# A graph-attention and mixture-of-experts layer: GpSimd normalises the rows of the first four routed blocks, and x is loaded in three pieces

## What is computed

```
sim  = tanh(adj * adj) where adj > 0            # adj is 4096 x 4096, float32
keep the 350 largest of each row of sim         # only rows with more than 350 positives change
h2   = tanh(layernorm(x) @ W_proj + b_proj)
x    = x + relu(new_adj @ (h2 @ W_gcn) + b_gcn)

n      = layernorm(x)
scores = n @ Wg.T + bg ; the two best experts ; softmax over their two scores
x      = x + sum over the two of  p_e * (relu(n @ W1[e].T + b1[e]) @ W2[e].T + b2[e])
```

## Time and profile before

| | us |
|---|---|
| runs | 513.41, 513.22, 513.01; median 513.22 |
| the profiled execution, its own time | 511.21 |
| its span | 509.4 |
| PE busy | 410.6 (81%) |
| DVE busy | 370.3 (73%) |
| ACT busy | 338.9 (67%) |
| POOL busy | 247.0 (48%) |

### The profile page before, as it was taken

The page is one execution under the profiler, slowest core; times in us unless marked ns, Lnnn a source line. Parts: engine busy times, 40 slices in busy tenths (PEclk is TensorE's granted clock), DMA queues, the critical chain, the costliest instruction groups (busy, mean ns, idle before and its releaser), DMA issues.

```text
span 509.4 us, 8989 instructions
## 1 busy us (share of the span) xinstructions
PE 410.6 (81%) x2671; PEld 256.7 (50%) x2672; DVE 370.3 (73%) x889; ACT 338.9 (67%) x345; POOL 247.0 (48%) x355
## 2 busy tenths in 40 slices
PE   0799999999898899999749999410999898989900
PEld 0455444444443445544334444210899898988900
DVE  4978899989999996696769999751555555554526
ACT  1789999799979876999757798100466555554500
POOL 2059941005206738718615875551266656564620
PEclk9999999999999999999978999855899999998975
DMA  8649589786666677586544781013233223232149
GB/s 242 266 146 378 219 286 374 251 283 245 222 243 213 227 264 284 188 292 272 196 181 129 278 314 69 31 43 121 77 88 96 82 62 92 64 86 65 40 155 339
DMA packets 31128, 95.56 MB, mean 188 GB/s; under 512 B 5532, under 2 KB 18132, under 8 KB 22896
## 3 DMA queue, kind: packets, MB, share of 16 engines
q1 hardware_dynamic: 19904, 80.06, 45.3%
q0 software_dynamic: 6048, 12.72, 7.5%
q10 hardware_dynamic: 5136, 2.30, 1.6%
HBM read 83.28 MB, written 12.67 MB: 188 GB/s over the span
## 4 chain that ended last, share of the span: by engine, by line
PE 21%; DVE 13%; issue 7%; DMA 4%; POOL 3%; SPq 2%; ACT 0%; POOLq 0%; DVEq 0%
DVE marks L820 5%; PE bank L1379 3%; PE bank L1380 3%; PE bank L1381 3%; PE bank L1400 3%; PE bank L1402 3%; PE bank L1401 3%; DMA tbuf<-expert_rows 2%; POOL expert_rows L602 2%; PE bank L1367 2%; POOL routed_rows L572 1%; DMA routed_rows<-aug,slots 1%; PE bank L1243 1%; SPq L422 1%; PE bank L1389 1%
## 5 line engine op out<-in xcount | busy, mean ns | idle before, releaser
L1269 PE MATMUL bank<-tbuf,g_sb 128*128 128x512 f32 x512 | 232.6, 602 | 1.7 <-ACT g_sb L1036 1.4
L1269 PEld LDWEIGHTS bank<-tbuf,g_sb 128*128 128x128 f32 x512 | 94.8, 192 | 108.9 <-issue 101.1
L820 DVE SCALAR_TENSOR_TENSOR marks<-abuf,marks 128x2048 bf16<-128x2048 int32 x56 | 128.3, 2291 | 1.2
L1016 ACT ACTIVATE tbuf<-abuf 128x2048 f32<-128x2048 f32 x64 | 121.4, 1897 | 3.5 <-PE bank L1269 2.7
L1020 ACT ACTIVATE tbuf<-tbuf 128x2048 f32<-128x2048 f32 x64 | 122.3, 1910 | 2.0
L602 POOL DMA_INDIRECT expert_rows<-abuf x78 | 76.7, 983 | 65.2 <-ACT abuf L1136 37.8
L572 POOL DMA_INDIRECT routed_rows<-aug,slots x64 | 83.7, 1308 | 50.4 <-DVE base L798 31.6
L982 DVE SCALAR_TENSOR_TENSOR tbuf<-bank,tbuf 128x512 f16<-128x512 f32 x78 | 51.8, 690 | 34.4 <-ACT tbuf L1130 34.4
L1130 ACT ACTIVATE tbuf<-bank 128x512 f16<-128x512 f32 x78 | 46.5, 597 | 44.5 <-PE bank L1381 43.1
L1400 PE MATMUL bank<-w2h,tbuf 128*128 x312 | 54.5, 220 | 0.0
L1401 PE MATMUL bank<-w2l,tbuf 128*128 x312 | 54.5, 220 | 0.0
(11 more groups left out here) (222 smaller groups left out, 510.8 us busy)
## 6 DMA issues: line engine op xcount, KB each, us to landing
abuf<-in_adj_tiles SPq DMA_DIRECT2D x64, 1024.0 KB, 5.2
abuf<-routed_rows SPq DMA_DIRECT2D x41, 130.0 KB, 2.1
wstage<-in_w POOLq DMA_DIRECT2D x16, 256.0 KB, 7.0
tbuf<-expert_rows SPq DMA_DIRECT2D x8, 512.0 KB, 6.9
out<-xres ACTq DMA_DIRECT2D x8, 256.0 KB, 6.2
expert_rows<-abuf POOLq DMA_INDIRECT x78
routed_rows<-pad SPq DMA_DIRECT2D x9, 130.0 KB, 2.5
routed_rows<-aug,slots POOLq DMA_INDIRECT x64
```

Of the source, the lines that this page charges most:

```text
L820: dve.scalar_tensor_tensor(mark, bits_in, 1.0, mark, ALU.min, ALU.add).then_inc(s_raw, 1)
L1016: act.activation(tbuf[:, n % NBUF, :, :], abuf[:, n % NBUF, :, :], ACT.Square).then_inc(s_sq, 1)
L1269: last = pe.matmul(ps_feat[ib % 2][:, :], g_sb[:, c, :], tbuf[:, buf, cc, :], start=(c == 0), stop=(c == C - 1))
```

## The change

Four edits are made.

- `normalise` and `cut_rows` take the engine as an argument. For the first four routed blocks GpSimd runs them, right behind `scale` of the same block and so ahead of `scatter` of the block before; for the last four blocks DVE runs them as before. Where DVE makes the scale itself (from the fifth block on) it first waits until the block before has been normalised.
- x is loaded in three pieces: 4, 8 and 20 column groups. The first two are issued ahead of adjacency chunk 0, the third behind it.
- At the start ACT and PE begin only group 0 ahead of chunk 0: ACT copies the turned group 0 ahead of the square of chunk 0 and its projection between square and tanh; PE turns only group 1 behind `gcn(0)`; `project(1)` and `turn_group(2)` stand behind chunk 0.
- The order of ACT's four small loads is changed (b_proj first), its table-loading activation reads `ident` and no longer waits for these loads, and PE waits for them only ahead of `project(0)`. A memset that only signals writes `need` in place of `tmp`, and `probabilities` gets the wait on the scatter of its `aug` buffer that `cut_rows` had on DVE.

```
-    PIECES = [(0, 3 * CK), (3 * CK, C)]
+    PIECES = [(0, CK), (CK, 3 * CK), (3 * CK, C)]
...
             load_x(0)
+            load_x(1)
             for n in range(NCH):
...
                 if n == 0:
-                    load_x(1)
+                    load_x(2)
...
             for i, b in enumerate(ORDER):
                 if i < POOLED:
                     scale(i, b, routed)
+                    normalise(pool, i, b, routed)
+                    cut_rows(pool, i, routed)
                 if i:
                     scatter(i - 1, routed)
...
                 if scale:
                     link(last)
+                    if i:
+                        dve.wait_ge(rs.xn, i)
                     last = norm_scale(dve, link, b * SUB, SUB)
...
             def probabilities(i, b, rs):
 
                 q = i % 2
+                if i >= 2:
+                    dve.wait_ge(rs.scat[q], i // 2 * Q * 16)
...
                     if n == START[i] + LATER[i] + AT_NORM:
-                        normalise(i, b, routed)
-                        cut_rows(i, routed)
+                        if i >= POOLED:
+                            normalise(dve, i, b, routed)
+                            cut_rows(dve, i, routed)
...
+            turned_out(0)
             square_chunk(0)
+            act.wait_ge(s_w, 64)
+            projected_out(0)
             tanh_chunk(0)
-            turned_out(0)
+            gcn_out(0)
             turned_out(1)
-            projected_out(0)
-            turned_out(2)
-            projected_out(1)
-            gcn_out(0)
...
+                if n == 0:
+                    projected_out(1)
+                    turned_out(2)
...
             turn_group(0)
+            pe.wait_ge(s_w, 64)
+            project(0)
+            gcn(0)
             turn_group(1)
-            project(0)
-            turn_group(2)
-            project(1)
-            gcn(0)
...
+                if n == 0:
+                    project(1)
+                    turn_group(2)
```

More of the change, by code:

```diff
@@ L382, in norm_scale, with normalise, cut_rows @@
             return last
+        def normalise(eng, i, b, rs):
+            eng.wait_ge(rs.ns, i + 1)
+            if i:
+                eng.wait_ge(rs.r2, i)
+                eng.wait_ge(rs.cut, 2 * i)
+            for cc in range(SUB):
+                c = b * SUB + cc
+                last = eng.tensor_scalar(nrm[:, cc, :], xres[:, c, :], mean[:, c:c + 1],
+                                         rstd[:, c:c + 1], ALU.subtract, ALU.mult)
+            last.then_inc(rs.xn, 1)
+        def cut_rows(eng, i, rs):
+            q = i % 2
+            if i >= 2:
+                eng.wait_ge(rs.scat[q], i // 2 * Q * 16)
+            if i == 0:
+                eng.wait_ge(s_one, 2)
+            eng.wait_ge(rs.xn, i + 1)
+            row = aug[:, q, 0, :, 0:D].bitcast(fp16)
+            eng.tensor_copy(row[:, :, 0:D - 1], nrm[:, :, 0:D - 1]).then_inc(rs.cut, 1)
+            eng.wait_ge(rs.cut, 2 * i + 1)
+            eng.tensor_tensor(row[:, :, D:2 * D - 1], nrm[:, :, 0:D - 1], row[:, :, 0:D - 1], ALU.subtract
+                              ).then_inc(rs.cut, 1)
         block = ctx.enter_context(nc.Block())
@@ L733, in add_features @@
                     link(last)
+                    if i:
+                        dve.wait_ge(rs.xn, i)
                     last = norm_scale(dve, link, b * SUB, SUB)
                 last.then_inc(rs.ns if scale else rs.st, 1)
-            def normalise(i, b, rs):
-                dve.wait_ge(rs.ns, i + 1)
-                if i:
-                    dve.wait_ge(rs.r2, i)
-                    dve.wait_ge(rs.cut, 2 * i)
-                for cc in range(SUB):
-                    c = b * SUB + cc
-                    last = dve.tensor_scalar(nrm[:, cc, :], xres[:, c, :], mean[:, c:c + 1],
-                                             rstd[:, c:c + 1], ALU.subtract, ALU.mult)
-                last.then_inc(rs.xn, 1)
-            def cut_rows(i, rs):
-                q = i % 2
-                if i >= 2:
-                    dve.wait_ge(rs.scat[q], i // 2 * Q * 16)
-                if i == 0:
-                    dve.wait_ge(s_one, 2)
-                dve.wait_ge(rs.xn, i + 1)
-                row = aug[:, q, 0, :, 0:D].bitcast(fp16)
-                dve.tensor_copy(row[:, :, 0:D - 1], nrm[:, :, 0:D - 1]).then_inc(rs.cut, 1)
-                dve.wait_ge(rs.cut, 2 * i + 1)
-                dve.tensor_tensor(row[:, :, D:2 * D - 1], nrm[:, :, 0:D - 1], row[:, :, 0:D - 1], ALU.subtract
-                                  ).then_inc(rs.cut, 1)
             def choose(i, b, rs):
@@ L883, in _ @@
                     write_features(early, 0)
-                    dve.memset(tmp[:, :], 0.0).then_inc(fixed_early, 1)
+                    dve.memset(need[:, :], 0.0).then_inc(fixed_early, 1)
                 for i, b in enumerate(ORDER):
@@ L941, in _ @@
                     add_features(b, b, rerouted, scale=True)
-                    normalise(b, b, rerouted)
-                    cut_rows(b, rerouted)
+                    normalise(dve, b, b, rerouted)
+                    cut_rows(dve, b, rerouted)
                     choose(b, b, rerouted)
@@ L1004, in _ @@
         def _(act):
+            act.dma_start(bp_sb[:, :], b_proj.rearrange("(p o) -> p o", o=1)).then_inc(s_w, 16)
             act.dma_start(wp_sb[:, :], w_proj).then_inc(s_w, 16)
             act.dma_start(wg_sb[:, :], w_gcn).then_inc(s_w, 16)
-            act.dma_start(bp_sb[:, :], b_proj.rearrange("(p o) -> p o", o=1)).then_inc(s_w, 16)
             act.dma_start(bg_sb[:, :], b_gcn.rearrange("(p o) -> p o", o=1)).then_inc(s_w, 16)
-            act.wait_ge(s_w, 64)
-            act.activation(ex[:, 0:1], bp_sb[:, 0:1], ACT.Tanh)
+            act.wait_ge(s_ident, 1)
+            act.activation(ex[:, 0:1], ident[:, 0:1], ACT.Tanh)
             def square_chunk(n):
@@ L1165, in _ @@
             pe.wait_ge(s_ident, 1)
-            pe.wait_ge(s_w, 64)
             def turn_group(g):
```

## The result

The changed kernel took 526.22 us (median of four, 523.79 to 529.38) where the kernel before took 513.12 beside it: a ratio of 1.026 (1.022 to 1.030), 13 us slower. I had said 513.6 and a range up to 517.0. The profiled execution took 525.71 with a span of 523.9, 14.5 more than before.

The account below looks back on a forecast made before the run. The stage was taken as often bound by DVE up to 320 us, with start, first two blocks and scatter deciding: -1.2 - 1.8 + 3.4 = +0.4, so 513.6 us as median; range 511.2 to 517.0.

Parts of the forecast that it names:

- the third block: Third routed block: forecast to change nothing, DVE spending its gained 4.43 wait on the next wait, for ACT's corrected rows.
- The start: Loading x in three pieces: -1.2 us at DVE's first mark, bounds +0.6 and -3.7.
- The price of normalising: GpSimd's four 128 x 128 operations, priced from a 0.29 us row: 1.2 us a block.
- my bound of 1.4 times: Upper bound on the forecast prices of GpSimd's pieces: a factor of 1.4 above.
- rival A: First two blocks: the last normalising operation runs into a mark if one takes over 0.4; 518.8 us, chance 0.15.
- The cast and the subtraction: GpSimd's cut of the rows: cast forecast at 0.6 us, subtraction of 1024 at 1.1 us.
- The relief of VectorE: First two blocks: of 2.72 us of relief DVE keeps 0.9 in each, -1.8 for both.
- just in time: First two blocks: ACT, 2.5 later at the cut, waited 2.50 at L1073 before, so it loses nothing.
- rival B: First two blocks: ACT binds, DVE's relief is lost on its wait for the cut; 515.4 us, chance 0.2.
- The fourth block: GpSimd's third-block scatter queues behind the fourth block's work: last issue and landing +3.4 us, bounds +2.2 and +5.0.
- The sign that I had named: At the scatter: ACT's long wait would grow from 9.2 to over 12 us.
- Rival C: Start gains about 2.2 and the marks miss the scatter (+2.4): 511.6 us, chance 0.2.

Follow-up runs that it names:

- e8: Changed kernel with GpSimd's four normalising operations replaced by affine_select over the same tiles, so rows are not normalised; ratio 1.010 to the kernel before.
- e12: Changed kernel with 24 spare products on TensorE ahead of its wait for normalised rows in the first two routed blocks; ratio 1.019 to the kernel before.
- e4: Changed kernel with the cut back on VectorE for all blocks, GpSimd only normalising the first four; ratio 1.011 to the kernel before.
- e16: Changed kernel with one added wait: in the first four routed blocks VectorE waits for GpSimd's normalised rows; ratio 1.019 to the kernel before.
- a2: The changed kernel itself, run again as reference on another chip; ratio 1.032 to the kernel before.
- e2: Kernel before with its old start, but GpSimd normalises and cuts the first four blocks; ratio 1.025 to the kernel before.
- e7: Changed kernel with normalising, turn and all that follows one step later for the first two routed blocks; ratio 1.020 to the kernel before.
- e9: Changed kernel with GpSimd's normalising tensor_scalar using two constants in place of mean and rstd, so rows are not normalised; ratio 1.019 to the kernel before.

## Why the prediction was wrong

**What bounds the kernel** was read rightly: the start, the first two blocks and the scatter are the three places where time moved, and the third block cost nothing.

**The start**: -1.2 forecast, -2.1 measured. The piece landed at 4.51 (4.6 forecast), and the first mark came at 28.86, 1.67 earlier than before. The rest was gained at the weights: behind the 3.92 wait GpSimd's loads came earlier by the lead, as I had said. The step is sound, its size 0.9 short. That the weight circle can throw it off by +4 or more I had not seen.

**The price of normalising** is the step that failed: "the nearest row is 0.29 us for a 128 x 128 operation". It was near in elements and not in kind. It is 0.79, and my bound of 1.4 times was much too tight. My own rows could have warned me: 1.2 for GpSimd's four is what VectorE takes for them (1.11), while for cast and subtraction I had GpSimd at 1.4 times VectorE or more (0.6 for the 0.43 of the earlier trace rows). And the trace of before has a nearer row than the one that I took, `tensor_scalar` itself over 128x128, with constants, begun in the last 0.24 us of a mark (timeline of GpSimd, before):

```profile
33.91 0.41 POOL L495 TENSOR_SCALAR fold<-ident 128x128 f32<-128x128 f32 x1
```

It is too low as well, but at 0.41 each the condition of my own rival A is met. The cast and the subtraction were right (0.61 and 1.15 for 0.6 and 1.1): they had rows of their own kind. e8 shows that it is this step, since with the operation of 0.29 us the first two blocks are near nothing. It is a near thing even so: the last of its four began 0.05 us ahead of the mark (135.89 and 135.94).

**What it set off** was in rival A, and too small there too. I had the mechanism, an operation that runs into the mark, and the condition, over 0.4 each; it had a chance of 0.15 and a price of 518.8. Two things made it 526. The operation that meets the mark is the second, with two more of 0.79 behind it, so the rows came 5.3 later against their block and not 3.5. And I had left out what an idle TensorE costs afterwards, 2.8 and 1.6 us by e12, though the front part shows its clock falling in the kernel before, at 260 us. The parts of the first block's 6.5 can be read from the runs: some 2 are left without the collision (2.1 in e4, 1.9 in e16), and 3.7 without the clock's fall (the 3.1 of e12 and the 0.6 by which its rows were earlier). Collision and clock are not two separate terms: the collision lengthens the idle time, and that is what lets the clock fall so far.

**The relief of VectorE**, -0.9 a block, did not come even with the cheap operation: -0.1 and +0.7 (e8). This is a second wrong step, and it does not hang on the price. In e8's first block, put on the clock of before (2.54 less), TensorE counts at 137.7 and ScalarE has the cut at 137.5, where the forecast had 137.5 for both. VectorE is 0.47 ahead (0.9 forecast), at the count's result and still at the old L775. But ScalarE, which lost 2.4 at the cut, is back at the old L1073 at 146.12, which began at 146.20 before. I had called this "just in time" and booked no loss; just in time is its old time, so VectorE's lead ends there. That is rival B's mechanism, at my own price. So of the forecast of -1.8 for two blocks nothing was there to win.

**The fourth block** reads as a hit (+3.4 and +3.4) and is two errors that cancel. With the forecast's own price (e8) the last issue moved by 3.5, as worked out, but the block cost 1.2, since the landing took 2.29 and not 4.59. With the real price the issue moved by 5.6 and the landing gave 2.15 back. I had moved the landing with the issue and not asked what else the DMA engines carry at the new place. The sign that I had named, ScalarE's long wait grown from 9.2 to over 12, did not show: it is 9.22 against 9.16, because ScalarE comes to it later itself, held 2.44 for the turned rows and 0.68 for the cut.

**Rival B** (the cut binds ScalarE) did not happen in the changed kernel, where TensorE's lateness covers it: 0.2 us of wait. In e8 it did, as said. **Rival C** had the start's 2.2 right, and the marks did not miss the scatter.

The Trainium skill, SBUF — State Buffer, section "SBUF: two separate sides", has an exclusive lock for whoever starts first. By that rule an operation begun ahead of the mark would have been safe. Two-input operations of GpSimd bear it out. In the changed kernel its subtraction L570 began 0.38 ahead of a mark and kept its time, and the mark took 4.21 for the usual 2.29 (timeline of GpSimd and VectorE, after):

```profile
52.01 2.44 POOL L570 TENSOR_TENSOR b_f<-b_f,b_h 2x1024 f32<-2x1024 f32 x1
...
52.39 4.21 DVE L827 SCALAR_TENSOR_TENSOR marks<-abuf,marks 128x2048 bf16<-128x2048 int32 x1
```

With the normalising `tensor_scalar` the traces do not follow it. Begun 0.01 to 0.06 us ahead of the mark it was held, all seven times (the changed kernel, a2, e2, e7: 2.89 to 2.94 us). Begun 0.30 to 0.73 ahead it kept its 0.79, but the mark was not stretched either, as in the second block of the changed kernel (175.11 and 175.43; 0.79 and 2.29). And the trace of before had shown that a lead is no safety, in L546, a `tensor_scalar` with one pointer that began 0.37 ahead of the mark of 56.27 and yet ended 0.90 behind the end of that mark:

```profile
55.90 3.55 POOL L546 TENSOR_SCALAR b_f<-b_f,is_p 2x1024 f32<-2x1024 f32 x1
```

Here the measurement decides: for this form a short lead over the mark does not help. Why it differs from the two-input forms is open.

## What to carry to other kernels

Price an operation on another engine from a row of the same form (the kind of operation and of operands), not of the same size; if the price comes out at what the faster engine takes for it, suspect it. Work given to GpSimd beside long VectorE operations should end before the next of them starts, or VectorE had better wait: 3.7 us of standing at an added wait were worth 8 us in total here. Ask of each relief which engine hands it on: one that arrives "just in time" passes nothing on. And a wait of TensorE can count twice, once for itself and once for the clock that it comes back with.

## What the runs showed of the hardware

- On GpSimd, 128x128 float32: `affine_select` 0.29 us, `tensor_scalar` with two constants 0.64 in e9 and 0.41 at L495, with two per-partition pointers 0.79 (VectorE: 0.34). `tensor_tensor` over 128x512 with one operand broadcast along the row takes 1.04, so two wide operations do in 2.16 what four `tensor_scalar` with pointers do in 3.14.
- TensorE's granted clock was at 0.50 behind an idle time of 6.7 us, and at 1.00 again by 144 us; eight products took 6.00 and 3.68 us at either level. Of idle times of 2.2 to 3.5 us one cost nothing and others 0.9 to 1.6.
- Beside a VectorE mark of 2.29 us a GpSimd operation of 0.79 that began with it took 2.89 to 2.94 and the mark kept its time. A GpSimd subtraction that had begun 0.38 ahead made the mark take 4.21, and a wide one made a VectorE operation of 0.16 take 0.89.
- The landing of a scatter issued on GpSimd took 4.59 us with the DMA engines at 79% and 2.44 at 13%.
- Of chips on which the first stage takes the same time to 0.2 us, one took 29 us more for the expert stage (509.4 against 539.1 us of span). What does it was not looked into.
